# Expert loop of a hybrid layer stack: row stores released by the next down products, row numbers converted by VectorE, four slots' addresses read by one load

## What is computed

```
def _swiglu(x, gw, uw, dw):
    return jax.nn.silu(x @ gw) * (x @ uw) @ dw
shared_out = _swiglu(x, shared_gate_w, shared_up_w, shared_down_w)
logits = x @ gate_w
topk_ids = jnp.argmax(logits, axis=-1)          # one of 32 experts for each token
topk_val = jnp.max(logits, axis=-1)
xs = x * jax.nn.sigmoid(topk_val)[:, None]
order = jnp.argsort(topk_ids)
g = _grouped_mm(xs[order], routed_gate_w, tokens_per_expert)
u = _grouped_mm(xs[order], routed_up_w, tokens_per_expert)
d = _grouped_mm(jax.nn.silu(g) * u, routed_down_w, tokens_per_expert)
return shared_out + d[jnp.argsort(order)]
```

## Time and profile before

| | us |
|---|---|
| median of three runs | 605.82 |
| lowest and highest of the three | 602.80, 606.84 |
| the profiled execution | 604.41 |
| its span, first to last instruction | 602.6 |
| stretches with the expert loop | about 166 to 229 and 530 to 591 |

### The profile page before, as it was taken

One profiled execution on the slowest core, in us unless ns is written; L12 is line 12 of the kernel. 1 busy time (PEld: TensorE's weight loads), 2 busy tenths in 40 slices (PEclk: granted clock), 3 DMA queues, 4 the chain that ended last, 5 costly groups with the idle time before them and its releaser, 6 DMA issues.

```text
span 602.6 us, 17012 instructions
## 1 busy us (share of the span) xinstructions
PE 527.8 (88%) x6418; PEld 309.6 (51%) x6418; DVE 430.9 (72%) x931; ACT 283.6 (47%) x608; POOL 273.9 (45%) x346
## 2 busy tenths in 40 slices
PE   6988978885889989999999999999999766889990
PEld 3323323443543334577767777777766644534330
DVE  3396599988255554888888888998789898245652
ACT  4633443452166651656645554566454242156650
POOL 3467666736426662333344443343322445416661
PEclk9999899998899998999999999999999887799996
DMA  5898900001637844000000000000000000617845
GB/s 169 358 426 159 107 1 2 0 4 34 206 87 218 231 125 123 15 15 20 20 21 21 20 20 21 23 23 21 13 20 8 7 6 31 206 53 221 244 142 156
DMA packets 45329, 54.14 MB, mean 90 GB/s; under 512 B 10880, under 2 KB 36416, under 8 KB 44224
## 3 DMA queue, kind: packets, MB, share of 16 engines
q1 hardware_dynamic: 42688, 47.78, 28.2%
q0 software_dynamic: 2560, 5.26, 2.5%
HBM read 43.55 MB, written 9.48 MB: 88 GB/s over the span
## 4 chain that ended last, share of the span: by engine, by line
PE 65%; DVE 23%; issue 6%; ACT 2%; DMA 2%; POOL 1%; SPq 0%; DVEq 0%; POOLq 0%; ACTq 0%
PE psum L1216 8%; PE psum L1639 7%; PE psum L1621 7%; PE psum L1712 5%; PE psum L1232 4%; PE psum L1691 4%; PE psum L1223 3%; PE psum L1133 3%; PE psum L1142 3%; PE psum L1660 3%; DVE arena L757 2%; PE psum L1592 2%; PE psum L274 2%; DVE arena L751 2%; PE psum L275 2%
## 5 line engine op out<-in xcount | busy, mean ns | idle before, releaser
L2100 POOL TENSOR_TENSOR arena<-arena 128x512 f32<-128x512 f32 x32 | 40.4, 1285 | 112.5 <-issue 103.9
L1412 POOL DMA_INDIRECT y_tok<-arena,to x48 | 56.3, 1173 | 60.5 <-ACT arena L1280 55.8
L1806 ACT ACTIVATE arena<-psum 128x512 f32<-128x512 f32 x64 | 38.1, 597 | 47.3 <-PE psum L1621 44.3
L1621 PE MATMUL psum<-arena 128*128 128x512 f32 x128 | 59.2, 605 | 0.7 <-ACT arena L1789 0.7
L1216 PE MATMUL psum<-experts,arena 128*32 x96 | 50.0, 603 | 1.9 <-issue 0.9
L1216 PE MATMUL psum<-arena 128*32 128x512 f32 x288 | 50.9, 605 | 0.0
L657 POOL TENSOR_TENSOR arena<-arena 128x512 f32<-128x512 f32 x32 | 37.2, 1181 | 27.8 <-DVE arena L757 17.5
L1347 DVE COPY arena<-psum 128x256 f32<-128x256 f32 x48 | 20.4, 424 | 40.7 <-PE psum L1223 39.7
L1639 PE MATMUL psum<-arena 128*128 128x128 f32 x384 | 47.5, 278 | 0.8 <-ACT arena L1811 0.8
L1285 ACT ACTIVATE arena<-experts 128x768 f32 x48 | 40.4, 845 | 13.2 <-issue 13.0
L1639 PEld LDWEIGHTS psum<-arena 128*128 128x128 f32 x384 | 45.2, 192 | 1.8 <-ACT arena L1811 1.8
(11 more groups left out here) (237 smaller groups left out, 1212.0 us busy)
## 6 DMA issues: line engine op xcount, KB each, us to landing
arena<-in_experts SPq DMA_DIRECT2D x48, 384.0 KB
experts<-in_experts SPq DMA_DIRECT2D x8, 1536.0 KB, 17.3
arena<-sorted_x SPq DMA_DIRECT2D x48, 64.5 KB
sorted_x<-zeros SPq DMA_DIRECT2D x2, 1536.0 KB, 14.6
arena<-in_w_qkv SPq DMA_DIRECT2D x16, 192.0 KB, 2.7
arena<-y_tok SPq DMA_DIRECT2D x8, 256.0 KB, 3.6
x_tok<-in_x SPq DMA_DIRECT2D x4, 256.0 KB, 3.9
arena<-in_w_out SPq DMA_DIRECT2D x16, 64.0 KB, 1.9
```

The source lines that it names most:

```text
L1412: pool.indirect_dma_start(out=y_tok, out_offset=bass.IndirectOffsetOnAxis(ap=f_to[:, s:s + 1], axis=0), in_=f_gy[s % 4], in_offset=None).t ...
L1621: pe.matmul(ring("in", n, j)[:, :], b_w[n % 2][:, which * P:which * P + P], x, start=True, stop=True)\
L1806: act.activation((b_q, b_k)[which][:, part * CHUNK:part * CHUNK + CHUNK], src, ACT.Copy, scale=(D_B ** -0.5, 1.0)[which]).then_inc(h["drai ...
L2100: pool.tensor_tensor(b_yn[:, part], b_y[:, part], b_rec[:, part], ALU.mult).then_inc(h["normed"], 1)
```

## The change

- `down` on TensorE no longer waits for `y_copied`, but for the last two slots. `gate_up` no longer waits for the copies of weights but for the first slots (two of ScalarE's, three of VectorE's).
- TensorE, ScalarE and VectorE read the addresses of four slots at once (`values_load_multi_w_load_instructions`), at every fourth slot. For this `f_slot_at` is written in the order of the four sides, 24 integers each. TensorE's read now stands behind the turning of the next rows. SyncE still reads one at a time.
- VectorE copies weights three slots ahead instead of two, and takes `address` over from GpSimd, at the end of its turn.
- GpSimd's indirect store of slot s waits in addition for `y` of slot s + 1 (all but the last).

```diff
@@ f_pe
             def find(s):
-                expert_at[s] = pe.value_load(f_slot_at[0:1, SIDE * s:SIDE * s + 1], min_val=0, max_val=(EXPERTS - 1) * WROW)
+                _, values = nc.values_load_multi_w_load_instructions(
+                    f_slot_at[0:1, s:s + FOUND], [pe.engine], min_val=0, max_val=(EXPERTS - 1) * WROW)
+                expert_at.update(zip(range(s, s + FOUND), values))
...
             def gate_up(s):
                 done(pe, "gxt", s + 1)
-                done(pe, "w_act", s + 1)
-                done(pe, "w_dve", s + 1)
+                if s < 2:
+                    done(pe, "w_act", s + 1)
+                if s < 3:
+                    done(pe, "w_dve", s + 1)
...
             def down(s):
                 done(pe, "sht", s + 1)
-                done(pe, "y_copied", s - 1)
+                if s >= RUNS - 2:
+                    done(pe, "y_copied", s - 1)
...
             for s in range(-1, RUNS + 2):
-                if 0 <= s < RUNS:
-                    find(s)
                 if s + 1 < RUNS:
                     turn_in(s + 1)
+                if 0 <= s < RUNS and s % FOUND == 0:
+                    find(s)
@@ f_act
             def copy_weights(s):
+                if s % FOUND == 0:
+                    find(s)
                 done(act, "y", s - 4)
-                at = act.value_load(f_slot_at[0:1, SIDE * s + 1:SIDE * s + 2], min_val=0, max_val=(EXPERTS - 1) * WROW)
-                act.activation(f_w_act[s % 5], experts[:, bass.ds(at, WROW)], ACT.Copy).then_inc(t["w_act"], 1)
+                act.activation(f_w_act[s % 5], experts[:, bass.ds(expert_at[s], WROW)], ACT.Copy).then_inc(t["w_act"], 1)
@@ f_dve
-            dve.tensor_copy(f_slot_at[0:1, :], f_slot_row[0:1, :]).then_inc(t["rows"], 1)
+            dve.tensor_copy(f_slot_at[0:1, :].rearrange("o (j s) -> o s j", j=SIDE), f_slot_row[0:1, :].rearrange("o (s j) -> o s j", j=SIDE)).then_inc(t["rows"], 1)
...
+            def address(s):
+                dve.wait_ge(slot_in[s % 8], 16 * (RUNS // 8 * k + s // 8 + 1))
+                dve.tensor_copy(f_to[:, s:s + 1], f_gx[s % 8][:, C:ROW]).then_inc(t["to"], 1)
...
-            for s in range(2):
+            for s in range(3):
                 copy_weights(s)
             for s in range(0, RUNS + 1):
                 if s >= 1:
                     copy_h(s - 1)
                 if s < RUNS:
                     product(s)
-                if s + 2 < RUNS:
-                    copy_weights(s + 2)
+                if s + 3 < RUNS:
+                    copy_weights(s + 3)
+                if s < RUNS:
+                    address(s)
@@ f_pool
-            for s in range(2):
-                address(s)
             for s in range(RUNS):
-                if s + 2 < RUNS:
-                    address(s + 2)
                 done(pool, "to", s + 1)
                 done(pool, "y_copied", s + 1)
+                if s + 1 < RUNS:
+                    done(pool, "y", s + 2)
                 pool.indirect_dma_start(out=y_tok, out_offset=bass.IndirectOffsetOnAxis(ap=f_to[:, s:s + 1], axis=0),
                                         in_=f_gy[s % 4], in_offset=None).then_inc(returned[s % 4], 16)
```

More of the change, by code:

```diff
@@ L49 @@
 RUNS = SLOTS * SLOT_ROWS // P
+FOUND = 4
 ROW = C + 1
@@ L1280, in copy_y, with find @@
                 act.activation(f_gy[s % 4], bank[6 + s % 2][:, 0:C], ACT.Copy).then_inc(t["y_copied"], 1)
+            expert_at = {}
+            def find(s):
+                _, values = nc.values_load_multi_w_load_instructions(
+                    f_slot_at[0:1, RUNS + s:RUNS + s + FOUND], [act.engine], min_val=0, max_val=(EXPERTS - 1) * WROW)
+                expert_at.update(zip(range(s, s + FOUND), values))
             def copy_weights(s):
+                if s % FOUND == 0:
+                    find(s)
                 done(act, "y", s - 4)
-                at = act.value_load(f_slot_at[0:1, SIDE * s + 1:SIDE * s + 2], min_val=0, max_val=(EXPERTS - 1) * WROW)
-                act.activation(f_w_act[s % 5], experts[:, bass.ds(at, WROW)], ACT.Copy).then_inc(t["w_act"], 1)
+                act.activation(f_w_act[s % 5], experts[:, bass.ds(expert_at[s], WROW)], ACT.Copy).then_inc(t["w_act"], 1)
             done(act, "rows", 1)
@@ L1347, in copy_h, with find @@
                 dve.tensor_copy(f_sht[s % 2], bank[4 + s % 2][:, 0:INNER]).then_inc(t["sht"], 1)
+            def address(s):
+                dve.wait_ge(slot_in[s % 8], 16 * (RUNS // 8 * k + s // 8 + 1))
+                dve.tensor_copy(f_to[:, s:s + 1], f_gx[s % 8][:, C:ROW]).then_inc(t["to"], 1)
+            expert_at = {}
+            def find(s):
+                _, values = nc.values_load_multi_w_load_instructions(
+                    f_slot_at[0:1, 2 * RUNS + s:2 * RUNS + s + FOUND], [dve.engine], min_val=0, max_val=(EXPERTS - 1) * WROW)
+                expert_at.update(zip(range(s, s + FOUND), values))
             def copy_weights(s):
+                if s % FOUND == 0:
+                    find(s)
                 done(dve, "y", s - 4)
-                at = dve.value_load(f_slot_at[0:1, SIDE * s + 2:SIDE * s + 3], min_val=0, max_val=(EXPERTS - 1) * WROW)
-                dve.tensor_copy(f_w_dve[s % 5], experts[:, bass.ds(at, WROW)]).then_inc(t["w_dve"], 1)
+                dve.tensor_copy(f_w_dve[s % 5], experts[:, bass.ds(expert_at[s], WROW)]).then_inc(t["w_dve"], 1)
             done(dve, "rows", 1)
             dve.wait_ge(loaded_experts, 16 * EXPERT_LOADS)
-            for s in range(2):
+            for s in range(3):
                 copy_weights(s)
@@ L1399, in f_pool @@
             scatter(pool, k, range(HALF_TILES, TILES))
-            def address(s):
-                pool.wait_ge(slot_in[s % 8], 16 * (RUNS // 8 * k + s // 8 + 1))
-                pool.tensor_copy(f_to[:, s:s + 1], f_gx[s % 8][:, C:ROW]).then_inc(t["to"], 1)
-            for s in range(2):
-                address(s)
             for s in range(RUNS):
-                if s + 2 < RUNS:
-                    address(s + 2)
                 done(pool, "to", s + 1)
                 done(pool, "y_copied", s + 1)
+                if s + 1 < RUNS:
+                    done(pool, "y", s + 2)
                 pool.indirect_dma_start(out=y_tok, out_offset=bass.IndirectOffsetOnAxis(ap=f_to[:, s:s + 1], axis=0),
@@ L1423, in weights @@
                 done(sp, "y", s - 5)
-                at = sp.value_load(f_slot_at[0:1, SIDE * s + 3:SIDE * s + 4], min_val=0, max_val=(EXPERTS - 1) * WROW)
+                at = sp.value_load(f_slot_at[0:1, 3 * RUNS + s:3 * RUNS + s + 1], min_val=0, max_val=(EXPERTS - 1) * WROW)
                 sp.dma_start(f_w[s % 6], w["experts"][:, bass.ds(at, WROW)]).then_inc(w_slot[s % 6], 16)
```

## The result

| kernel | median, us | runs (lowest to highest) |
|---|---|---|
| before | 603.83 | 20 (601.52 to 607.20) |
| after | 607.67 | 20 (603.93 to 612.84) |

The ratio is 1.0071, with a 95% interval of 1.0050 to 1.0092: slower by 0.7%, under the 1% that was set as the bound of no change, but clearly not the gain of 0.4% to 0.7% that was forecast (601.4 us), and just above the top of the range (607.0). The forecast started from a median of three runs, 605.82; over twenty runs the same kernel takes 2.0 us less. The profiled execution after has a span of 605.7 us, against 602.6.

A forecast was written before the change was run, and what follows sets the result against it. Signals held during GpSimd's indirect row stores were taken as the bound. First pass -2.5, second -1.1, together -3.6; one slipped signal made it -4.4, from the median 605.82 to 601.4 us; range 594.5 to 607.

The forecast's parts named there:

- the cover of the batch: TensorE's four-address read lies under the held signal, 0.83 us of cover a turn: cost zero, 0.3 a batch at the upper end.
- held turn: Loop turn set by signals held while GpSimd makes store descriptors: 2.37 us before, 2.07 to 2.18 after, 2.15 taken.
- The chain: A pass ends with row stores on GpSimd, then gathers; whatever moves the 24th store's start moves the kernel.
- the one signal that was to slip through: One down signal in the two passes meets the gap in the hold and spares about 0.8 us.
- The size of the batch: Reading four addresses at once costs TensorE 3 x 0.28 = 0.84 us per batch; ScalarE and VectorE hide theirs.
- The 0.68: Gain at the start of each pass, since no address read stands ahead of TensorE's gate/up there any more: 0.68 us.
- the 0.92: First row store of a pass, now waiting for the second down products, less the start's gain: 0.92 us later.
- The last two stores 1.26 apart: At a pass's end stores 23 and 24 wait for the same down products, so the 24th follows 1.26 us later.
- Store and weight copy: Rival: GpSimd's store and VectorE's weight copy collide each turn, turn 2.71 us, kernel 626 us; chance 0.10.
- the batch isn't covered: Rival: TensorE pays the batch itself, 3 us on top of the held turn, 604.4 us; batch or no gain 0.19.

The follow-up runs named there:

- after_look: The changed kernel, unchanged, run on another chip without held signals: 601.88 us, ratio 1.0255 to the kernel before on that chip.
- own_release: The changed kernel with GpSimd's new wait for the next slot's down products taken out: 599.62 us, ratio 1.0189 to the kernel before.
- eight_reads: The changed kernel with reads of eight addresses at a time instead of four: 617.08 us, ratio 1.0508 to the kernel before.

## Why the prediction was wrong

In short: the cover of the batch failed. The four checks of a batch were counted at nothing since a held turn would hide them; they cost 0.9 us at the start of each pass, where nothing is held, and 1.2 us of TensorE's time at every fourth slot behind it, where four held turns have no more than that to spare.

*The chain (stores on GpSimd, then gathers), and the end of a pass as the place to measure:* right for most of it; the passes are longer by 2.3 and 2.1 us.

*The held turn:* it came on the first chip nearly in the forecast size. ScalarE's timeline after, copies of down products, and the down products ahead of the first two on TensorE:

```profile
197.40 0.28 ACT L1286 ACTIVATE arena<-psum 128x128 f32<-128x128 f32 x1 [0.42 <-PE psum L1238]
...
199.59 0.28 ACT L1286 ACTIVATE arena<-psum 128x128 f32<-128x128 f32 x1
...
201.80 0.28 ACT L1286 ACTIVATE arena<-psum 128x128 f32<-128x128 f32 x1 [0.34 <-PE psum L1238]
```

```profile
196.22 0.28 PE L1238 MATMUL psum<-arena 128*32 128x128 f32 x3
...
199.25 0.28 PE L1238 MATMUL psum<-arena 128*32 128x128 f32 x3
```

The copies of 197.40 and 201.80 are held: they come 1.44 and 1.46 after the stores of 195.96 and 200.34, the first 0.9 after its products' end (196.50). Each store starts 0.75 after the start of the copy that the same signal released (197.40 to 198.15, 199.59 to 200.34). 0.75 + 1.45 = 2.20. Forecast were 0.73 and 1.34 to 1.45, and 2.15 was taken. No copy in the two passes started less than 1.31 after the store before it, so the one signal that was to slip through, and spare 0.8, didn't.

But only about two turns in four are held turns. The copy of 199.59 isn't held: it starts 0.06 after its products' end (199.53), which comes late because TensorE's batch stood ahead of it; that this is 1.44 after a store too is chance. And in each four one copy is late by ScalarE's own batch (up to 1.4 us after its products' end).

*The size of the batch:* nearly right for TensorE (0.84 forecast, 0.76 measured). The term missed what the same read does to ScalarE and VectorE: both were to hide theirs, but cost 0.39 together.

*The cover of the batch:* this step failed. It was counted at nothing since the hold leaves 0.83 us of slack in a turn.

At the start of a pass no store has run and nothing is held, so nothing covers it; the prediction put a gain of 0.68 there and no cost. Measured, the first gate/up comes 1.1 us later (171.17 against 170.07), of which 0.2 lie ahead of the pass. From the last addition it is 2.92 us against 2.00, and 2.68 against 1.82 in the second pass. The runs on other chips tell whose it is: 2.88 with three batches, 2.90 with TensorE's alone, 1.99 with single reads, 1.73 unchecked. In the first pass the lower clock after that idle time costs 1.5 us more (the first two steps are 1.69 and 2.57 us, on the other chip, at the full clock, 1.26 and 1.47). It did not come in the second pass, nor in either pass of after_look, so it is no fixed price of the change. The 0.68 did come, with the 0.92 of which it was part: 0.92 + 1.10 + 1.53 = 3.55, and the first store is 3.58 later. The batch of the fifth slot then makes the second store follow by 3.00, 0.8 more than a held turn.

In the held part no single turn hides a batch. TensorE, which no longer waits for the copy of the result, takes 1.91 us for three turns and 2.7 to 3.6 for the fourth, 3.09 in the mean over ten, where the chip without held signals has 3.06. What the hold could give is the sum over four turns: 4 x 2.20 = 8.8 us, against TensorE's 3 x 1.91 + 3.0 = 8.7 at best, and 8.9 and 9.0 in the means of the two passes. The pace of the stores behind the second (16 turns of 2.22 and 2.24 us) is that of TensorE's gate/ups. With the 2.15 and the 0.84 of the forecast the four turns would have been 8.6 and 8.5, just enough; both terms were somewhat larger, and the margin was gone.

The sum for the first pass, from the forecast of the last store at 225.57 to 230.53: 2.66 at the first store, 20 x (2.257 - 2.15) = 2.13 in the turns, 0.17 at the end, together 4.96. Second pass, 589.69 to 593.39: 1.45, 2.38 and -0.13, together 3.70. Of these, 0.2 and 0.5 were there before the pass began. Of the 2.13 and 2.38 about 0.8 is the second store and 1.0 the held turn of 2.20 for 2.15.

*The last two stores 1.26 apart:* right (229.26 and 230.53: 1.27).

*Store and weight copy:* right that they don't collide. VectorE's timeline of the change:

```profile
198.11 0.63 DVE L1378 COPY arena<-experts 128x768 f32 x1
...
200.61 0.55 DVE L1378 COPY arena<-experts 128x768 f32 x1
```

The copy of 198.11 and the store of 198.15 start together; the store takes 0.96, the copy 0.63 where the next, which starts 0.27 into a store, takes 0.55. All 48 stores have 0.96 in the mean, where before they had 1.17. The Trainium skill (SBUF — State Buffer, Who interferes with whom) has the two exclude each other for the whole instruction; the trace disagrees for this order.

*The rival "the batch isn't covered"* came nearest: it named the mechanism and the row that would show it (a gap of over 0.5 before each fourth gate/up) and gave 604.4. Its sum took 0.3 a batch on top of the held turn and left out the start of the pass.

*What the forecast could not know:* on five of six chips the signals aren't held. The gain was to come from a shorter hold, and where there is none the batch stands bare, at 14 us. That the held signals on the first chip are due to GpSimd's making of descriptors is argued from rows of that chip and not shown, nor that they are a lasting property of it; single reads or the later release alone were not run there, so whether either gains on it stays open.

## What to carry to other kernels

A read of several register values at once saves loads and not checks: count the instructions that it issues on the sequencer, on every engine that does it, and place them where something longer runs. Work that is spread over turns and fits a small slack in each can cost more when it is gathered into one turn, above all ahead of the first work of a loop, where nothing covers it. And slack that comes from a stall (here a held signal) is no cover to build on: it may be gone on the next chip.

## What the runs showed of the hardware

- On one chip of six, ScalarE's copies started 0.59 to 0.75 or 1.32 to 1.49 us after an indirect store began, up to 1.17 us after the end of the products that they waited for, and none between. On another chip a copy started inside a store, 0.14 us after its products' end. The same kernel takes 603.8 and 588 us on them.
- A check of a value's bounds, with its assertion, takes about 0.3 us of TensorE's sequencer, of which the two instructions show 0.15 and 0.02. The load takes 0.30 for one value, 0.33 for four, 0.60 for eight.
- After 1.48 us (own_release, second pass), 1.72 us (the change, first chip) and 2.33 us (eight_reads) of idle TensorE its matmuls ran at the lower clock (1.2 GHz; 1.06 us for 0.61); after 1.68 us in the profile of the change on another chip they didn't (0.61, granted clock 1.00), nor after 1.48 us in the second pass of the change on the first chip. The idle time alone doesn't tell.
- The same wait on GpSimd costs nothing as the first of three and 0.5% as the last; the store starts 0.30 to 0.32 us after the end of what it waits for in the one case and 0.81 to 0.83 in the other.
